# Softplus's correction on GpSimd, max(x, 0) and the 1 of Ln(1 + e) on ScalarE, in a two-layer kernel with a selective scan

## What is computed

```python
x_dbl = u @ x_proj_w.T                       # R + N + N = 64 + 16 + 16 columns
dt = rmsnorm(x_dbl[..., :R], dt_ln_w)        # x * rsqrt(mean(x^2) + 1e-6) * w
Bm = rmsnorm(x_dbl[..., R:R + N], b_ln_w)
Cm = rmsnorm(x_dbl[..., R + N:], c_ln_w)
dt = softplus(dt @ dt_proj_w.T + dt_proj_b)  # 256 channels
dA = exp(dt[..., None] * A)                  # A: 256 x 16
dBu = (dt * u)[..., None] * Bm[:, :, None, :]
h = dA_t * h + dBu_t                         # over the 512 tokens, for each of 16 states
y = einsum('lbin,bln->bli', h_seq, Cm) + u * D
```

## Time and profile before

| | us |
|---|---|
| median of 3 runs | 1080.19 (1080.01 to 1082.65) |
| span of the profiled execution | 1078.4 |
| TensorE matmuls busy | 874.0 (81%) |
| VectorE busy | 804.8 (75%) |
| ScalarE busy | 640.1 (59%) |
| GpSimd busy | 415.1 (38%) |
| chain that ended last: TensorE / VectorE / issue / GpSimd | 41% / 30% / 13% / 10% |

### The profile page before, as it was taken

The page is one execution under the profiler, slowest core; times in us unless marked ns, Lnnn a source line. Parts: engine busy times, 40 slices in busy tenths (PEclk is TensorE's granted clock), DMA queues, the critical chain, the costliest instruction groups (busy, mean ns, idle before and its releaser), DMA issues.

```text
span 1078.4 us, 14023 instructions
## 1 busy us (share of the span) xinstructions
PE 874.0 (81%) x4458; PEld 487.2 (45%) x4458; DVE 804.8 (75%) x1059; ACT 640.1 (59%) x1969; POOL 415.1 (38%) x241
## 2 busy tenths in 40 slices
PE   1743988886888897989797989797979896889785
PEld 0511767673533463446343634363336333534443
DVE  7665344566878887897789778978797879877466
ACT  0231546562768466856685568556855685678464
POOL 2266122115553256235623562346224632553000
PEclk9957999998999899999999999999999999999898
DMA  7463878973432263325332523253325332541000
GB/s 231 139 191 99 246 234 263 300 208 88 119 89 59 62 169 83 72 62 164 79 81 61 158 72 90 66 154 71 91 66 134 75 93 71 163 101 21 21 11 11
DMA packets 85945, 123.09 MB, mean 114 GB/s; under 512 B 8560, under 2 KB 43760, under 8 KB 85744
## 3 DMA queue, kind: packets, MB, share of 16 engines
q1 hardware_dynamic: 79584, 115.38, 38.4%
q0 software_dynamic: 6288, 6.82, 2.8%
HBM read 106.21 MB, written 12.29 MB: 110 GB/s over the span
## 4 chain that ended last, share of the span: by engine, by line
PE 41%; DVE 30%; issue 13%; POOL 10%; ACT 4%; DMA 2%; SPq 0%; DVEq 0%; POOLq 0%
PE y_bank L1279 11%; DVE hst L801 10%; DVE dBu L793 5%; POOL hc L1190 3%; POOL xs_d L1158 3%; PE work L1297 3%; PE more L1398 3%; POOL x_res L1174 3%; DVE nmax L946 2%; PE work L1444 2%; PE work L1380 2%; DVE dc L863 2%; PE work_l L1380 1%; PE work L1410 1%; DVE fsg L955 1%
## 5 line engine op out<-in xcount | busy, mean ns | idle before, releaser
L1190 POOL TENSOR_TENSOR hc<-hst,bcr 128x1024 f32<-128x1024 f32 x116 | 277.6, 2393 | 507.2 <-DVE dBu L793 447.8
L1279 PE MATMUL y_bank<-hc,pk 128*128 128x512 f32 x512 | 261.4, 635 | 61.6 <-POOL hc L1190 48.1
L801 DVE TENSOR_TENSOR_SCAN hst<-dA,dBu 128x1024 f32<-128x1024 f32 x128 | 291.5, 2278 | 14.5 <-issue 12.6
L793 DVE TENSOR_TENSOR dBu<-dtu,bcr 128x1024 f32<-128x1024 f32 x128 | 176.3, 1377 | 15.4 <-DMA bcr<-bc_d 2.0
L1016 ACT ACTIVATE dA<-dt,neg_a 128x511 f32<-128x511 f32 x256 | 171.1, 727 | 9.3 <-DVE hst L801 8.0
L1279 PEld LDWEIGHTS y_bank<-hc,pk 128*128 128x128 f32 x512 | 92.3, 195 | 161.5 <-issue 77.9
L1101 ACT COPY pT<-more 96x512 f32<-96x512 f32 x120 | 69.8, 582 | 87.8 <-PE more L1398 87.6
L1398 PE MATMUL more<-pk,pexp 128*96 128x128 f32 x480 | 94.2, 292 | 21.0 <-ACT pexp L1088 16.2
L1398 PEld LDWEIGHTS more<-pk,pexp 128*96 128x96 f32 x480 | 57.8, 130 | 90.3 <-issue 71.2
L1088 ACT ACTIVATE pexp<-work,nmax 128x96 f32<-128x96 f32 x240 | 78.2, 339 | 15.4 <-DVE nmax L946 15.4
L1088 ACT ACTIVATE pexp<-work_l,nmax 128x96 f32<-128x96 f32 x240 | 78.1, 339 | 4.0 <-DVE nmax L946 3.8
(11 more groups left out here) (355 smaller groups left out, 1465.2 us busy)
## 6 DMA issues: line engine op xcount, KB each, us to landing
bcr<-bc_d SPq DMA_DIRECT2D x128, 512.0 KB
qbd<-in_wx SPq DMA_DIRECT2D x8, 578.0 KB, 4.7
o_all<-in_wx SPq DMA_DIRECT2D x8, 578.0 KB, 4.6
pT<-in_wx SPq DMA_DIRECT2D x8, 578.0 KB
kT<-in_wx SPq DMA_DIRECT2D x8, 578.0 KB, 5.1
vw<-in_wx SPq DMA_DIRECT2D x8, 578.0 KB, 5.0
xs_d<-rbuf POOLq DMA_DIRECT2D x1, 2560.0 KB, 9.7
hst<-in_hidden SPq DMA_DIRECT2D x8, 256.0 KB, 6.7
```

What stands on the lines that cost most here:

```text
L793: v.tensor_tensor(dBu[:], dtu[par], bcr[n % RING][:, 0:1, :].to_broadcast([P, NH, L]), ALU.mult).then_inc(s_dBu, 1)
L801: v.tensor_tensor_scan(hst[n % 2][:].rearrange("p h t -> p (h t)"), dA[n % 2][:].rearrange("p h t -> p (h t)"), dBu[:].rearrange("p h t -> ...
L1190: g_.tensor_tensor(hc[n % 2][:], hst[n % 2][:], bcr[n % RING][:, 1:2, :].to_broadcast([P, NH, L]), ALU.mult).then_inc(s_hc, 1)
L1279: last = t.matmul(y_bank[h][:], ident, hc[n % 2][:, h, :], start=False, stop=(n == N - 1))
```

## The change

- PRE_AT loses `drl0` and `drl1`; `de` moves from slot 22 to 20, `dw` from 23 to 21, `dln` from 24 to 22, `dt` from 25 to 23.
- ScalarE: behind each Abs a Relu with bias makes `drl` and frees the bank; the Ln reads e and adds 1 by its bias, so that it waits for the Exp alone.
- GpSimd does units `dw` and `dt` for sequences 1 to 7: w - 1, e - (w - 1), + Ln, + `drl`. For sequence 0 VectorE does them, in the same form. The tile `dc` is gone.
- GpSimd makes `ms` by two small operations ahead of `rr`, and `var` by one ahead of `rstd`; VectorE's four small ones are gone.

```diff
-PRE_AT = {... 18: ['dtp0'], 19: ['drl0', 'dtp1'], 21: ['drl1'], 22: ['de'], 23: ['dw'], 24: ['dln'], 25: ['dt'], 26: ['dtu'], 27: ['start']}
+PRE_AT = {... 18: ['dtp0'], 19: ['dtp1'], 20: ['de'], 21: ['dw'], 22: ['dln'], 23: ['dt'], 26: ['dtu'], 27: ['start']}
...
@@ VectorE
-                    dve.wait_ge(s_ss, b * 6 + 3)
-                    for k, w in enumerate((R, N, N)):
-                        v.tensor_scalar(ms[:, :, k], ss[:, :, k], 1.0 / w, RMS_EPS, ALU.mult, ALU.add).then_inc(s_ss, 1)
...
-                elif name in ("drl0", "drl1"):
-                    h = int(name[3:])
-                    dve.wait_ge(s_dab, b * NH + h + 1)
-                    v.tensor_scalar(drl[:, h, :], bank0[:], pc("dt_b")[:, h:h + 1], 0.0,
-                                    ALU.add, ALU.max).then_inc(s_free0, 1)
-                elif name == "dw":
-                    dve.wait_ge(s_de, b + 1)
-                    v.tensor_scalar(dw, de, 1.0, None, ALU.add).then_inc(s_dw, 1)
-                    dve.wait_ge(s_dw, b + 1)
-                    v.scalar_tensor_tensor(dc[:], dw, -1.0, de, ALU.add, ALU.subtract).then_inc(s_dc, 1)
-                elif name == "dt":
-                    dve.wait_ge(s_dc, b * 2 + 1)
-                    dve.wait_ge(s_dln, b + 1)
-                    v.tensor_tensor(dc[:], dln, dc[:], ALU.subtract).then_inc(s_dc, 1)
-                    dve.wait_ge(s_dc, b * 2 + 2)
-                    v.tensor_tensor(dt[par], dc[:], drl, ALU.add).then_inc(s_dt, 1)
+                elif name == "dw" and b == 0:
...
-                    v.tensor_scalar(var1[:], mv1[:, :, 1], LN_EPS, None, ALU.add).then_inc(s_stat1, 1)
@@ ScalarE
                     s.activation(dab[:, h, :], bank0[:], ACT.Abs, bias=pc("dt_b")[:, h:h + 1]).then_inc(s_dab, 1)
+                    s.activation(drl[:, h, :], bank0[:], ACT.Relu, bias=pc("dt_b")[:, h:h + 1]).then_inc(s_free0, 1)
...
-                    act.wait_ge(s_dw, b + 1)
-                    s.activation(dln, dw, ACT.Ln).then_inc(s_dln, 1)
+                    act.wait_ge(s_de, b + 1)
+                    s.activation(dln, de, ACT.Ln, bias=one[:]).then_inc(s_dln, 1)
@@ GpSimd
-                        pool.wait_ge(s_ss, b * 6 + 6)
+                        pool.wait_ge(s_ss, b * 3 + 3)
+                        g_.tensor_tensor(ms[:], ss[:], pc("rms_n").unsqueeze(1).to_broadcast([P, NT, 3]),
+                                         ALU.mult).then_inc(s_ms, 1)
+                        pool.wait_ge(s_ms, b * 2 + 1)
+                        g_.tensor_scalar(ms[:], ms[:], RMS_EPS, None, ALU.add).then_inc(s_ms, 1)
+                        pool.wait_ge(s_ms, b * 2 + 2)
...
+                    elif name == "dw" and b > 0:
+                        pool.wait_ge(s_de, b + 1)
+                        g_.tensor_scalar(dw, de, 1.0, -1.0, ALU.add, ALU.add).then_inc(s_dw, 1)
+                        pool.wait_ge(s_dw, b * 3 + 1)
+                        g_.tensor_tensor(dw, de, dw, ALU.subtract).then_inc(s_dw, 1)
+                    elif name == "dt" and b > 0:
+                        pool.wait_ge(s_dln, b + 1)
+                        pool.wait_ge(s_dw, b * 3 + 2)
+                        g_.tensor_tensor(dw, dw, dln, ALU.add).then_inc(s_dw, 1)
+                        done0(pool, b, "dtp1")
+                        pool.wait_ge(s_dw, b * 3 + 3)
+                        g_.tensor_tensor(dt[1 - par], dw, drl, ALU.add).then_inc(s_dt, 1)
...
+                        g_.tensor_scalar(var1[:], mv1[:, :, 1], LN_EPS, None, ALU.add).then_inc(s_rstd1, 1)
+                        pool.wait_ge(s_rstd1, b * 3 + 1)
                         g_.tensor_tensor(rstd1[:], var1[:], minus_half[:, 0:NT], ALU.pow).then_inc(s_rstd1, 1)
```

More of the change, by code:

```diff
@@ L70 @@
 FFN_AT = {12: 0, 17: 1, 21: 2}
-PRE_AT = {0: ['xnT', 'hs0'], 2: ['u0'], 3: ['hs1'], 4: ['zg0', 'u1'], 6: ['sg0', 'zg1'], 7: ['sg1'], 9: ['xdbl'], 10: ['ss'], 12: ['xdr'], 13: ['bc'], 16: ['dtT'], 18: ['dtp0'], 19: ['drl0', 'dtp1'], 21: ['drl1'], 22: ['de'], 23: ['dw'], 24: ['dln'], 25: ['dt'], 26: ['dtu'], 27: ['start']}
+PRE_AT = {0: ['xnT', 'hs0'], 2: ['u0'], 3: ['hs1'], 4: ['zg0', 'u1'], 6: ['sg0', 'zg1'], 7: ['sg1'], 9: ['xdbl'], 10: ['ss'], 12: ['xdr'], 13: ['bc'], 16: ['dtT'], 18: ['dtp0'], 19: ['dtp1'], 20: ['de'], 21: ['dw'], 22: ['dln'], 23: ['dt'], 26: ['dtu'], 27: ['start']}
 LAYER1_AT = {0: ['out'], 1: ['x1'], 2: ['ln_a'], 3: ['ln_b'], 4: ['q', 'k'], 5: ['v0', 'v1'], 6: ['v2'], 7: ['v3'], 27: ['rden']}
@@ L289, in program @@
         bcr = [sb(f"bcr{k}", [P, 2, L]) for k in range(RING)]
-        dc = sb("dc", [P, NH, L])
+        conv_half = sb("conv_half", [P, I])
         z = [sb(f"z{k}", [P, NH, L]) for k in range(2)]
@@ L435, in program @@
         s_dw = sem("dt_w_ready")
-        s_dc = sem("dt_c_ready")
+        s_ms = sem("mean_squares_ready")
         s_dln = sem("dt_ln_ready")
@@ L680, in _ @@
                                    ALU.mult, ALU.mult).then_inc(s_const, 1)
-            rest = dc[:, 0, 0:I]
+            rest = conv_half[:]
             v.memset(conv_rows[:], 0.0).then_inc(s_cbias, 1)
@@ L848, in pre @@
                         last.then_inc(s_free0 if k == 2 else s_xdr, 1)
-                elif name in ("drl0", "drl1"):
-                    h = int(name[3:])
-                    dve.wait_ge(s_dab, b * NH + h + 1)
-                    v.tensor_scalar(drl[:, h, :], bank0[:], pc("dt_b")[:, h:h + 1], 0.0,
-                                    ALU.add, ALU.max).then_inc(s_free0, 1)
-                elif name == "dw":
-                    dve.wait_ge(s_de, b + 1)
-                    v.tensor_scalar(dw, de, 1.0, None, ALU.add).then_inc(s_dw, 1)
-                    dve.wait_ge(s_dw, b + 1)
-                    v.scalar_tensor_tensor(dc[:], dw, -1.0, de, ALU.add, ALU.subtract).then_inc(s_dc, 1)
-                elif name == "dt":
-                    dve.wait_ge(s_dc, b * 2 + 1)
-                    dve.wait_ge(s_dln, b + 1)
-                    v.tensor_tensor(dc[:], dln, dc[:], ALU.subtract).then_inc(s_dc, 1)
-                    dve.wait_ge(s_dc, b * 2 + 2)
+                elif name == "dw" and b == 0:
+                    dve.wait_ge(s_de, 1)
+                    v.tensor_scalar(dw, de, 1.0, -1.0, ALU.add, ALU.add).then_inc(s_dw, 1)
+                    dve.wait_ge(s_dw, 1)
+                    v.tensor_tensor(dw, de, dw, ALU.subtract).then_inc(s_dw, 1)
+                elif name == "dt" and b == 0:
+                    dve.wait_ge(s_dln, 1)
+                    dve.wait_ge(s_dw, 2)
+                    v.tensor_tensor(dw, dw, dln, ALU.add).then_inc(s_dw, 1)
                     done0(dve, b, "dtp1")
-                    v.tensor_tensor(dt[par], dc[:], drl, ALU.add).then_inc(s_dt, 1)
+                    dve.wait_ge(s_dw, 3)
+                    v.tensor_tensor(dt[par], dw, drl, ALU.add).then_inc(s_dt, 1)
                 elif name == "dtu":
@@ L907, in layer1 @@
                         v.bn_stats(stats1[:, j, :], x1r[par][:, j, :]).then_inc(s_stat1, 1)
-                    dve.wait_ge(s_stat1, b * 10 + 4)
+                    dve.wait_ge(s_stat1, b * 9 + 4)
                     v.memset(tick[:], 0.0)
@@ L911, in layer1 @@
                         v.bn_aggr(mv1[:, j, :], stats1[:, j, :]).then_inc(s_stat1, 1)
-                    dve.wait_ge(s_stat1, b * 10 + 8)
-                    v.tensor_scalar(var1[:], mv1[:, :, 1], LN_EPS, None, ALU.add).then_inc(s_stat1, 1)
+                    dve.wait_ge(s_stat1, b * 9 + 8)
                     v.tensor_scalar(shift1[:], mv1[:, :, 0], -1.0, None, ALU.mult).then_inc(s_stat1, 1)
@@ L1029, in pre @@
                     full0(act, b, name)
-                    before(act, s_dc, 2 * b)
                     s.activation(tg[:, h, :], bank0[:], ACT.Tanh).then_inc(s_tg, 1)
@@ L1033, in pre @@
                     full0(act, b, name)
-                    before(act, s_ss, b * 6)
+                    before(act, s_ss, b * 3)
                     s.activation(xsq[:], bank0[:, 0:NT * XW].rearrange("p (j c) -> p j c", c=XW),
@@ L1056, in layer1 @@
                 if name == "ln_b":
-                    act.wait_ge(s_rstd1, b * 2 + 2)
+                    act.wait_ge(s_rstd1, b * 3 + 3)
                     for j in range(NT):
```

4 lines of the change are left out of this document (2 added, 2 removed).

## The result

The changed kernel takes 1087.61 (1086.93 to 1089.21, six runs), the one before 1080.10 (1079.39 to 1084.43, six runs): a ratio of 1.0051, 95% interval 1.003 to 1.0073. It is slower by more than the 0.3% that can be told from no change; the forecast was 1073, with 1084 as the upper end. The profiled executions have spans of 1078.4 and 1087.1.

A forecast was written before the change was run, and what follows sets the result against it. No engine was taken to bound a whole turn; GpSimd's new chain limited the gain. Six full turns gave -3.6, the two end turns +0.5, the experts' turn -4.0: -7.1 from 1080.2, say 1073, range 1061 to 1084.

The forecast's parts named there:

- `ms` in slot 10, +0.4 a turn: First norm: two small GpSimd operations and their waits ahead of `rr`, less 0.25, delay the path by 0.4 in each full turn.
- The exclusion: VectorE gets operations such as `dBu` done only after GpSimd has stopped; scans and row maxima, which read PSUM, run unharmed.
- `dw` 1.5, bounds 0.95 and 2.35: GpSimd's first softplus operation takes 1.5, between a memset of that size, 0.95, and a two-input product, 2.35.
- Softplus's stretch, -1.25: Full turns: with the correction off VectorE, step 14's `hc` releases TensorE's last y sum; gating comes at 685.5 instead of 686.74.
- The ceiling of 5.2: Most a full turn could gain in softplus's stretch: 17.0 us behind the last softplus against 22.2.
- `dBu` 14 not blocked: VectorE's `dBu` of step 14, wanted at 667.8, finds GpSimd's subtraction ended at 667.5; it waits 0.5 with `dw` at 2.35.
- `dBu` 15 blocked: VectorE's `dBu` of step 15 queues with GpSimd's addition and `dt`, blocked for 1 to 4 us a turn.
- Second norm, +0.25: One small GpSimd operation put before `rstd`, with VectorE's `shift` waiting for `hc`, costs 0.25 a turn.
- Turn with the experts, -4.0: VectorE loses `ms` 1.98, `dc` and `dt` 1.24 + 1.23 ahead of an expert's output: -4.45; Relus return 0.45.
- Turns 7 and 8, +0.5: The two turns at the end have the second norm's cost alone, together +0.5.
- ScalarE, +0.95: A Relu of 0.69 and exponential of 1.06 enter 0.80 idle before the gate's Tanh, delaying it and scan 13 by 0.95.
- The rival for slower: GpSimd's four long softplus operations contend, 0.58 more each; full turns +1.7, time 1087; chance 0.15.

## Why the prediction was wrong, step by step

- **`ms` in slot 10, +0.4 a turn.** Its own size was right: the two operations and their gaps, less 0.25, make `tick_p` 0.38 later behind `hc` 6 (5.21 for 4.83). Measured is +1.40. What failed is the sentence that all of it is passed on as it is; the prediction looked for what VectorE would lose through `rr`, and never at what GpSimd has between `rr` and the gathers, nor when VectorE's `dBu` starts. The exclusion that its first part describes was applied to long operations alone. It holds for one element and for the issue of a gather too. The kernel with nothing moved and GpSimd 0.47 late shows it without `ms`: +1.24. Since VectorE lost its own `ms`, the `dBu` came 0.21 earlier as well, and the margin of 0.51 was used up from both ends.
- **No term for the clock.** The prediction has the 4.29 and the wait of TensorE behind `hc` 7, but not the y sum's 3.18 for 1.98, which stood in the row behind the pause. Filled, the pause gives back 0.6% in the changed kernel (ratios 1.0051 and 0.9992) and 1.0% in the one before. All of the +3.69 from 7 to 9 belongs here, since filled the stretch is 64.9 in both kernels.
- **`dw` 1.5, bounds 0.95 and 2.35.** Measured 3.64, above the upper bound, and above the 2.4 that the prediction itself named as a sign of being wrong. The bound took for granted that one input is not slower than two. `dt` took 3.14, since VectorE's `dBu` 15 got in ahead of it, as the 1.2 in the sum had it.
- **Softplus's stretch, -1.25.** Measured (-2.66)/6 = -0.44 with the two falls of the clock before, and -0.10 without them. `hc` 13 to `hc` 14 is 7.90, for 7.78 before and 8.4 forecast; the slip lies ahead of `hc` 13, where `dw` is 2.1 longer than taken. Counted from `hc` 12, `hc` 14 ends at 19.94 (686.39), where 18.79 was forecast, and the gating follows it by 5.53, forecast 5.55. So the mechanism held and the longer `dw` ate the gain: `hc` 14 releases step 14's y sum, the gating is not released by VectorE's last `hc`, and the gain is a small part of the 6.8 us removed. (The ceiling of 5.2 is three quarters of these 6.8, not two thirds; nothing else uses that.)
- **`dBu` 14 not blocked.** Wrong, 2.77: behind the longer `dw` the subtraction was still running when `dBu` wanted to start. **`dBu` 15 blocked** was right.
- **Second norm, +0.25.** Right in size: (2.47 - 1.18)/6 = +0.22.
- **Turn with the experts, -4.0.** Measured -2.4. Kernels with `ms` on VectorE have 140.2 to 141.7 from the first `hc` to turn 1's; those with `ms` alone or both norms on GpSimd 137.7 and 137.6, so moving `ms` gave -3.4, more than its 1.98. The 2.47 for `dc` and `dt` did not come: the steps are on GpSimd's side of the ring now, `hc` 12 to `hc` 14 took 16.80 for 16.24 (15.98 with `ms` alone), with the `dBu` blocked 2.33 at 221.13.
- **Turns 7 and 8, +0.5.** Measured -0.1, in a stretch that varies by 4 over the kernels, so the term can't be judged.
- **ScalarE, +0.95.** Nearly right. ScalarE's timeline has the Tanh 6.78 behind the second Abs before, and 668.49 - 660.98 = 7.51 behind it now, +0.73; scan 13 starts 4.45 behind `hc` 12, for 3.34. What this costs a turn by itself no run shows. Before, then after:

```profile
662.48 0.60 ACT L1104 ACTIVATE fth<-work 128x512 f32<-128x512 f32 x1 [0.28 <-PE work L1410]
```

```profile
668.49 0.61 ACT L1094 ACTIVATE fth<-work 128x512 f32<-128x512 f32 x1
```

Added up, from the forecast of -7.1 to the measured span of +8.7: `ms` and its followers 6.0, the clock from 7 to 9 3.7, softplus's stretch 4.9, the turn with the experts 1.6 and the first `hc` 1.35, less 0.9 from 9 to 12, 0.6 in turns 7 and 8 and 0.2 in the second norm. The first `hc` stands at 126.0 to 130.2 over all kernels, so its part can't be put down to the change.

The rival for slower gave 1087, which is the time that came, but by luck and another way: it wanted contention among four long operations at 2.93 each, with the loss in softplus's stretch. The subtraction took 2.36 and the addition 2.35; `dt` took 3.14 with a wait for VectorE. The kernel with softplus alone on GpSimd was faster, not slower. The Trainium skill's rule that stood beside it (GPSIMD Engine Reference, 4.1 Engine selection: two-input work about twice as slow on GpSimd, one-input at about line rate) is right for the first half and not for the second: 2.35 to 1.23, and 3.64, or 2.80 in one step, to VectorE's 0.68.

## What to carry to other kernels

Before you put a small operation ahead of others on GpSimd, measure the distance of all that stands behind it to VectorE's next long operation on SBUF: up to it a delay costs itself; beyond it, it cost 0.8 to 1.0 us more here, for a single element or the issue of a gather. Read the row behind each pause of TensorE too: where it takes more than its fellows, the pause costs more than its length, and idle products that fill it can be worth more than the change. Judge a change with such a remedy only beside the old kernel with the same remedy. Split a change that has two parts before you judge it; here one part gained 5.0 and the other lost 10.0. And before you credit a gain, look whether the clock fell in other turns of the two profiles: 2.1 of the 2.66 here were that.
